# Ninth tap's projection inside the row-tile burst, and one TensorE loop over both axes, in an LSTM and deformable-sampling kernel

## The reference

```python
def dsc_axis(x, offset, weight, axis):
    off = jnp.transpose(offset, (0, 2, 3, 1))      # 9 offsets for each pixel
    if axis == 'x':
        ix = wb + off; iy = jnp.broadcast_to(hb, off.shape)
    else:
        iy = hb + off; ix = jnp.broadcast_to(wb, off.shape)
    s = grid_sample_zeros(x, ix, iy)               # linear between two pixels of the row or column
    return jnp.einsum('bchwk,ock->bohw', s, weight)
...
x = x + lstm_layer(_gn(x), ...)
x = x + conv_block(_gn(x), ...)
```

## Time and profile before

| | us |
|---|---|
| median of 3 runs | 934.19 (932.71 to 934.72) |
| the profiled execution, its own time | 935.11 |
| its span | 933.3 |
| TensorE busy, matmuls | 794.4 (85%) |
| TensorE busy, weight loads | 620.6 (66%) |
| VectorE busy | 635.0 (68%) |
| ScalarE busy | 522.8 (56%) |
| POOL busy | 114.3 (12%) |
| L868, `dist`, 4608 matmuls, busy | 219.8 |
| L914, `product`, 8192 matmuls (its further ones, with y8, are listed by themselves), busy | 194.2 |
| L881, `project`, 4096 matmuls, busy | 78.8 |
| L893, `project_last`, 2048 matmuls, busy | 67.6 |

### The profile page before, as it was taken

How to read it: one execution, slowest core, us unless ns; L and a number is a source line. 1 busy time by engine, 2 the same in 40 slices (tenths; PEclk the granted TensorE clock), 3 DMA queues, 4 the chain that set the end, 5 groups by cost and what they waited for, 6 DMA issues and landing times.

```text
span 933.3 us, 61844 instructions
## 1 busy us (share of the span) xinstructions
PE 794.4 (85%) x27560; PEld 620.6 (66%) x27560; DVE 635.0 (68%) x1472; ACT 522.8 (56%) x1044; POOL 114.3 (12%) x227
## 2 busy tenths in 40 slices
PE   0688888879779999779779999999979999999970
PEld 0455556555357777523468888889868888898860
DVE  4466666664622222377668888888868999999975
ACT  0344444440121111165668888888857888888854
POOL 0122222210000000000211111111111111111103
PEclk9999999985679999989999999999999999999995
DMA  8200000000000000000000000000000000000006
GB/s 213 81 2 1 0 1 0 0 1 1 3 2 4 4 4 4 3 2 1 3 3 0 0 0 0 0 0 0 1 5 1 0 0 0 0 0 0 0 3 180
DMA packets 4073, 12.15 MB, mean 13 GB/s; under 512 B 1391, under 2 KB 1787, under 8 KB 3460
## 3 DMA queue, kind: packets, MB, share of 16 engines
q1 hardware_dynamic: 1716, 4.88, 1.9%
q10 hardware_dynamic: 1522, 4.14, 1.6%
q0 software_dynamic: 768, 2.10, 0.8%
HBM read 6.92 MB, written 4.19 MB: 12 GB/s over the span
## 4 chain that ended last, share of the span: by engine, by line
PE 75%; DVE 11%; issue 6%; ACT 4%; DMA 2%; POOL 1%; ACTq 0%; DVEq 0%; POOLq 0%
PE psum L914 16%; PE psum L868 15%; PE psum L817 14%; PE psum L881 8%; PE psum L893 6%; PE psum L755 5%; PE psum L840 3%; PE psum L742 3%; DVE offs L637 2%; DVE wide L556 2%; PE psum L797 2%; DVE wide L559 2%; DMA xs<-in_x_dram 2%; ACT wide L382 1%; ACT wide L386 1%
## 5 line engine op out<-in xcount | busy, mean ns | idle before, releaser
L457 ACT ACTIVATE wide<-psum 128x512 f32<-128x512 f32 x576 | 304.0, 606 | 10.8 <-PE psum L868 10.7
L656 DVE TENSOR_SCALAR wide<-wide 128x512 f32<-128x512 f32 x576 | 246.6, 447 | 48.0 <-ACT wide L457 37.8
L868 PE MATMUL psum<-wide,sels 125*32 125x256 bf16 x4608 | 219.8, 275 | 4.2 <-issue 3.3
L914 PE MATMUL psum<-wide 128*32 128x64 f32 x8192 | 194.2, 219 | 9.4 <-issue 8.4
L914 PEld LDWEIGHTS psum<-wide 128*32 128x32 f32 x8192 | 168.5, 109 | 12.6 <-issue 11.0
L662 DVE COPY wide<-psum 128x512 f32<-128x512 f32 x192 | 131.5, 685 | 10.2 <-PE psum L881 10.1
L817 PE MATMUL psum<-img,offs 32*32 32x512 f32 x3456 | 126.7, 596 | 4.4 <-DVE img L610 4.4
L755 PEld LDWEIGHTS psum<-wide 128*64 128x64 f32 x2048 | 75.9, 140 | 66.5 <-issue 65.8
L817 PEld LDWEIGHTS psum<-img,offs 32*32 32x32 f32 x3456 | 96.0, 103 | 34.3 <-issue 7.9
L868 PEld LDWEIGHTS psum<-wide,sels 125*32 125x32 bf16 x4608 | 94.6, 97 | 25.3 <-issue 15.2
L755 PE MATMUL psum<-wide 128*64 128x64 f32 x2048 | 89.7, 229 | 21.7 <-DVE wide L567 19.4
(11 more groups left out here) (97 smaller groups left out, 821.2 us busy)
## 6 DMA issues: line engine op xcount, KB each, us to landing
xs<-in_x_dram SPq DMA_DIRECT2D x8, 256.0 KB, 9.8
xs<-in_x_dram ACTq DMA_DIRECT2D x8, 256.0 KB, 11.0
out_dram<-wide SPq DMA_DIRECT2D x16, 128.0 KB, 3.5
out_dram<-wide POOLq DMA_DIRECT2D x16, 128.0 KB, 4.0
offs<-in_cw_dram ACTq DMA_DIRECT2D x1, 576.0 KB
sels<-in_sel_dram ACTq DMA_DIRECT2D x1, 562.5 KB
wide<-in_dsc_dram ACTq DMA_DIRECT2D x1, 288.0 KB
offs<-in_dwd_dram ACTq DMA_DIRECT2D x1, 288.0 KB
```

The costliest lines, as they stand in the source:

```text
L457: nc.scalar.activation(hat_tile(par, i), ps[USE_BANK[u]].rearrange("p (q n) -> p q n", q=2), ACT.Abs).then_inc(d_read, 1)
L656: nc.vector.tensor_scalar(v, v, 1.0, 1.0, ALU.min, ALU.subtract).then_inc(v_ready, 1)
L868: last = mm(bank[c, e * SL:(e + 1) * SL], sels[:, k, c], oc[0:NROW, par, :], start=(e == 0), stop=(e == 1))
L914: last = mm(ps[O_BANK][C * q:C * q + C, cols], w, v, start=(group == 0), stop=(group == GROUPS - 1))
```

## The change

- `wm8` and `project_last` are gone. The ninth tap is now computed in `project`, in the same form as the other taps: weights are the pixels (64 columns), and the moving operand is the 32 columns of tap 8. There are 16 such matmuls (32 recorded) a slot, each 32 rows by 64 columns of the array. Groups 0 and 1 go in front of the other taps' matmuls of row tiles 0 and 1, groups 2 and 3 in front of those of row tiles 2 and 3. As groups 0 and 2 write the same partitions of the bank, and 1 and 3 likewise, TensorE waits for `y8_half`, the end of the first half, ahead of row tile 2.
- The ninth tap is use 0 (bank 0), the hats are uses 1 to 9. GROUPS_AFTER is new.
- ScalarE takes the ninth tap first, in two activations of 64 partitions by 256 columns, into alternate blocks of `y8`, then hat 0, then y of group 0, then hats 1 to 8. The blocks of `y8` that are never written are zeroed once by POOL at the start.
- TensorE's two loops are one of 31 rounds, for both axes, with two slots behind it. For this `project` always reads the weights of axis 0, and POOL, at the change of axis, waits until all slots of axis 0 are projected and copies the weights of axis 1 over them.

```diff
-        wm8 = region(2 * 2 * Q * C).rearrange("p (a e q n) -> p a e q n", a=2, e=2, q=Q)
...
-        USES, Y8_USE = 10, 4
+        USES, Y8_USE = 10, 0
...
+            nc.gpsimd.memset(y8[:, :, :, :, :], 0.0).then_inc(y8_zero, 1)
...
-            step(nc.gpsimd.memset(wm8, 0.0))
-            for a in range(2):
-                for q in range(Q):
-                    s_ = slice(C * q, C * q + C)
-                    last = nc.gpsimd.tensor_copy(wm8[s_, a, q % 2, q, :], wcv[s_, a, 8, :])
-            last.then_inc(wm_ready, 1)
-            pool.wait_ge(wm_ready, 1)
...
+                    if g0 == NCH:
+                        pool.wait_ge(y_ready, Q * 2 * NCH)
+                        step(nc.gpsimd.tensor_copy(wc[:, 0, :], wc[:, 1, :]))
...
+            act.wait_ge(y8_zero, 1)
             with act.Fori(0, 2 * NCH) as g:
                 for par in range(2):
-                    act.wait_ge(y_ready, g * (2 * Q) + (par * Q + 1))
-                    nc.scalar.activation(yt[:, par, 0, :, :], ps[Y_BANK[0]]..., ACT.Copy).then_inc(y_read_a, 1)
-                    for u in range(USES):
-                        if u == Y8_USE:
-                            act.wait_ge(y8_ready, g * 2 + (par + 1))
-                            nc.scalar.activation(y8[:, par, :, :, :], ps[USE_BANK[u]]..., ACT.Copy).then_inc(d_read, 1)
-                        else:
-                            ...
+                    act.wait_ge(y8_ready, g * 2 + (par + 1))
+                    for e in range(2):
+                        half = slice(S * e, S * e + S)
+                        last = nc.scalar.activation(y8[half, par, :, e:Q:2, :],
+                                                    ps[USE_BANK[Y8_USE]][half, 0:2 * HROWS * C].rearrange(
+                                                        "p (r q m) -> p r q m", r=HROWS, q=2), ACT.Copy)
+                    last.then_inc(d_read, 1)
+                    for i in range(HATS):
+                        act.wait_ge(d_ready, g * (2 * HATS) + (par * HATS + i + 1))
+                        nc.scalar.activation(hat_tile(par, i), ps[USE_BANK[hat_use(i)]]..., ACT.Abs).then_inc(d_read, 1)
+                        if i == 0:
+                            act.wait_ge(y_ready, g * (2 * Q) + (par * Q + 1))
+                            nc.scalar.activation(yt[:, par, 0, :, :], ps[Y_BANK[0]]..., ACT.Copy).then_inc(y_read_a, 1)
...
-            def project(a, s, slots, par):
+            def project(s, slots, par):
                 ...
+                free_bank(s, slots, Y8_USE)
                 for r in range(HROWS):
+                    pair = (0, 1) if r < 2 else (2, 3)
+                    if r == 2:
+                        pe.wait_ge(y8_half, s + (slots + 1))
+                    for r8 in (r * 2 % HROWS, r * 2 % HROWS + 1):
+                        for q in pair:
+                            c, e = slice(C * q, C * q + C), q % 2
+                            at = (2 * r8 + q // 2) * C
+                            last = mm(ps[USE_BANK[Y8_USE]][S * e:S * e + S, at:at + C], xc[c, par, r8 * S:(r8 + 1) * S],
+                                      wcv[c, 0, 8, :], start=(r8 == 0 and q < 2), stop=True, skip_group_check=True)
+                        if r8 == HROWS - 1:
+                            last.then_inc(y8_half if r < 2 else y8_ready, 1)
                     for e in range(2):
                         ...
-            def project_last(a, s, slots, par):
-                ...
-            GROUPS_AFTER = (0, 3, 3, 2, 1, 3, 3, 3, 2, 0)
+            GROUPS_AFTER = (0, 2, 2, 3, 2, 3, 2, 3, 3, 0)
...
-            pe.wait_ge(wm_ready, 1)
-            for a in range(2):
-                s0 = 2 * a * NCH
-                if a == 0:
-                    slot(a, s0, None, 1, True)
-                with pe.Fori(0, NCH - 1) as g:
-                    for par in range(2):
-                        slot(a, g * 2, s0 + par, par, True)
-                slot(a, 2 * NCH - 2, s0, 0, True)
-                slot(1, 2 * NCH - 2, s0 + 1, 1, a == 0)
+            slot(0, None, 1, True)
+            with pe.Fori(0, 2 * NCH - 1) as g:
+                for par in range(2):
+                    slot(g * 2, par, par, True)
+            slot(4 * NCH - 2, 0, 0, True)
+            slot(4 * NCH - 2, 1, 1, False)
```

More of the change, by code:

```diff
@@ L173, in build @@
                                                      for n in ("off_mm", "part1", "rest1", "part2", "rest2", "part3"))
-        wm_ready = sem("wm_ready")
+        y8_zero = sem("y8_zero"); y8_half = sem("y8_half")
         xc_ready = sem("xc_ready"); oc_ready = sem("oc_ready"); d_ready = sem("d_ready"); d_read = sem("d_read"); v_ready = sem("v_ready")
@@ L441, in _ @@
                 parts_x(rd)
+            act.wait_ge(y8_zero, 1)
             with act.Fori(0, 2 * NCH) as g:
                 for par in range(2):
-                    act.wait_ge(y_ready, g * (2 * Q) + (par * Q + 1))
-                    nc.scalar.activation(yt[:, par, 0, :, :], ps[Y_BANK[0]].rearrange("p (r m) -> p r m", r=HROWS),
-                                         ACT.Copy).then_inc(y_read_a, 1)
-                    for u in range(USES):
-                        if u == Y8_USE:
-                            act.wait_ge(y8_ready, g * 2 + (par + 1))
-                            nc.scalar.activation(y8[:, par, :, :, :],
-                                                 ps[USE_BANK[u]].rearrange("p (r q m) -> p r q m", r=HROWS, q=Q),
-                                                 ACT.Copy).then_inc(d_read, 1)
-                        else:
[L455 to L458, removed]
+                    act.wait_ge(y8_ready, g * 2 + (par + 1))
[7 more added lines that the diff above has]
+                        act.wait_ge(d_ready, g * (2 * HATS) + (par * HATS + i + 1))
+                        nc.scalar.activation(hat_tile(par, i), ps[USE_BANK[hat_use(i)]].rearrange("p (q n) -> p q n", q=2),
+                                             ACT.Abs).then_inc(d_read, 1)
+                        if i == 0:
+                            act.wait_ge(y_ready, g * (2 * Q) + (par * Q + 1))
+                            nc.scalar.activation(yt[:, par, 0, :, :], ps[Y_BANK[0]].rearrange("p (r m) -> p r m", r=HROWS),
+                                                 ACT.Copy).then_inc(y_read_a, 1)
             norm_sqrt(BNF, 1)
@@ L881, in project @@
                             last = mm(ps[Y_BANK[q]][S * e:S * e + S, r * P:(r + 1) * P], xc[c, par, r * S:(r + 1) * S],
-                                      wcv[c, a, e:8:2, :], start=(r == 0), stop=(r == HROWS - 1))
+                                      wcv[c, 0, e:8:2, :], start=(r == 0), stop=(r == HROWS - 1))
                             if e == 1 and r == HROWS - 1:
                                 last.then_inc(y_ready, 1)
-            def project_last(a, s, slots, par):
[L888 to L895, removed]
             GROUPS = HROWS * 5
-            GROUPS_AFTER = (0, 3, 3, 2, 1, 3, 3, 3, 2, 0)
+            GROUPS_AFTER = (0, 2, 2, 3, 2, 3, 2, 3, 3, 0)
             def product(s, slots, par, group):
@@ L916, in product, with slot @@
                     last.then_inc(out_ready, 1)
-            def slot(a, s, slots, par, ahead):
+            def slot(s, slots, par, ahead):
                 nslots = 0 if slots is None else slots + 1
@@ L923, in slot @@
                     pe.wait_ge(oc_ready, s + (nslots + 1))
-                    project(a, s, nslots, 1 - par)
+                    project(s, nslots, 1 - par)
                 for u in range(USES):
[L926 to L929, removed]
+                    if ahead and u != Y8_USE:
+                        dist(s, nslots, 1 - par, u - 1)
                     if slots is not None:
```

## The result

The changed kernel took 956.95 us in the median (948.42 to 963.38, 4 runs), the kernel before 934.46 (932.71 to 936.55, 4 runs). The recorded ratio is 1.016, 95% interval 1.0119 to 1.0202; in a second series on another chip it is 1.0353, 1.0255 to 1.0450. Executions fall on two levels some 14 us apart (before 933.5 or 920.3, after 963.3 or 949.5), and the recorded ratio compares the changed kernel's two executions at the lower level (950.65 and 948.42) with executions of the kernel before that are all at the upper one, whereas at one and the same level the change costs 29 to 30 us, 3.2%. The cleanest measure is the sampling itself, from the first burst's start to the last's: 442.87 us before, 470.13 after, +27.3; a second profile of the changed kernel gives 470.07. The profiled execution took 963.25 us against 935.11, +28.1.

The account below looks back on a forecast made before the run. TensorE and ScalarE were taken to be near the limit together, ScalarE's chain setting the new slot. 60 slots at +0.28 gave +16.8 us, one loop -11.7: together +5.1, 939.3 us against the median 934.19; range 914 to 952, forecast's own 931 to 947.

Parts of the forecast that it names:

- One loop, -11.7: At the change of axis, TensorE's stalls on the first pass through new code vanish with one loop: -11.7 us.
- The burst ends at 2.03 and grows by 0.82: TensorE's burst of ninth tap and `project`, at 57 ns a ninth-tap pass, ends at 2.03 us instead of 1.21.
- ScalarE starts the ninth tap at 1.84: ScalarE starts 1.84 us after the burst's start, when the last ninth-tap pass is done and seen.
- Each half activation takes 0.29, hat 0 starts at 2.42: ScalarE's two 256-column ninth-tap activations take 0.58 us in place of 0.50, so hat 0 can start at 2.42.
- Seven steps to hat 6, 3.36: On ScalarE, hat 0, the copy of y and hats 1 to 5 take 0.48 us each, 3.36 in all.
- Hat 6 itself 0.61: ScalarE's hat 6, which frees the bank for the last `dist`, takes 0.61 us.
- 0.33 from the last dist to the burst: At the slot's end, the next burst starts 0.33 us after the last `dist` starts.
- The moved waits: TensorE's `free_bank` ahead of the burst and `y_ready` behind hat 0 find their events past: cost 0.
- cheap passes: Rival: a ninth-tap pass costs its 27 ns of streaming, the burst grows by 0.37, 913.5 us; chance 27%.
- TensorE alone counts: Rival: ScalarE catches up, so TensorE's time sets the slot at 6.44 us, 919.5 us total; chance 10%.
- strict order: Rival: array tiles don't pass each other, the burst ends at about 2.2, slot 6.95, 949.5 us; chance 19%.
- The rule of program order: Skill's rule: TensorE matmuls stay in program order, only weight loads are pulled ahead; ninth-tap passes would hold back other tiles.

Follow-up runs that it names:

- after_again: The changed kernel run once more, unchanged, as the reference on the same chip: median 963.3 us, sampling 470.07 us.
- wide_tap: The changed kernel with 64 columns streamed in each ninth-tap matmul in place of 32: median 959.95 us, sampling 473.92 us.
- no_free: The changed kernel without the `free_bank` wait at the head of `project`: median 957.88 us, sampling 465.46 us.
- half_act: The changed kernel with only the first of the two ninth-tap activations, TensorE's work the same: median 951.01 us, sampling 458.12 us.
- spread_lean: The kernel before with one TensorE loop, two product groups moved behind the ninth tap's projection, and no wait for `oc` at the slot's head: median 925.99 us.

## Why the prediction was right and wrong

The direction and the mechanism were right, the size was not: +5.1 us was forecast and 28.1 measured in the profiled executions. The stated range of 914 to 952 held the recorded outcome (1.016 times 934.46 is 949.4), but that is luck: it hangs on which executions that ratio compares. The 963 us of the profiled execution and of `after_again` lie outside the range, and the forecast's own range of 931 to 947 held neither value. Step by step:

- *One loop, -11.7*: right. It is 11.70 alone, 11.0 of it at the change of axis. Undone in the changed kernel it is 8.7, so there the rest of the change costs 36 and not 39.
- *The burst ends at 2.03 and grows by 0.82*: right. It is 2.06, +0.85. `wide_tap` shows that the streamed columns are not the price of a pass; the weight load as the price fits but was not varied.
- *ScalarE starts the ninth tap at 1.84*: right, 1.85 (598.80 - 596.95).
- *Each half activation takes 0.29, hat 0 starts at 2.42*: this step failed. The second half starts 0.39 after the first (0.77 less its 0.38) and hat 0 0.40 after that, so hat 0 starts at 2.64, +0.22. I had taken off the overlap that activations of 512 columns show. What was measured, 0.39 and 0.40, is above even the upper bound of 0.375 that stood in the prediction. Why these halves do not overlap is open.
- *Seven steps to hat 6, 3.36*: right (599.59 to 602.95). *Hat 6 itself 0.61*: 0.67, +0.06. In the unbroken row hats start 0.48 apart but each ends a little later; their mean rose to 630 ns from 606.
- *0.33 from the last dist to the burst*: 0.41, +0.08. This step failed too. The moved waits were costed at nothing because their events are past. `no_free` shows what one of them costs anyway: an instruction of the sequencer, 0.07 to 0.10.
- These three terms are 0.36, and 6.78 + 0.36 = 7.14: the slot is explained to 0.01. Odd slots take 0.02 more. Over 60 slots (14.74 - 13.44) / 2 = 0.65 is 39 us; less 11.7 that leaves 27.3, the measured growth of the sampling.

Of the rivals, *cheap passes* fell with the burst and `wide_tap`; *TensorE alone counts* with `half_act`; *strict order* gave 949.5, the figure nearest to the recorded ratio, but by a burst of 2.2 that isn't there, so its nearness is luck as well. The rule of program order that the prediction took from the Trainium skill ("TensorE: Matmul & The Clock Gate", step-by-step part of Part 2) does not hold between tiles in this trace. The eight ninth-tap passes of a row tile stand ahead of the other taps' in the program, yet the first L894 starts at 597.09 while the last of these L887 start at 597.14. The sum that lets the tiles run past each other hit the burst to 0.03. What was foreseen of the two waits of TensorE, ahead of `dist` 4 and of the last `dist`, is in the profile.

The share of each cause follows from the chain, laid beside that of the kernel before (6.49 to 7.13). ScalarE starts its row 1.85 after the burst's start in place of 1.19, as it waits for the last ninth-tap pass of the longer burst: +0.66, the largest part. From there to the end of hat 6 it takes 4.82 in place of 4.92: -0.45 for the old stop ahead of the ninth tap, +0.29 for two activations in place of one, +0.06 for the longer hat 6. The path from there to the next burst is 0.07 longer. The sum is 0.63 of the 0.64. The prediction says that one step before hat 6 is gone; that is wrong, though its sum does not use it: the same eight pieces (the ninth tap, the copy of y, hats 0 to 5) stand ahead of hat 6 in both kernels.

## What to carry to other kernels

Two engines that hand banks to each other can both be near the limit: take the slot apart from the event that closes it, back to the burst, and price a change on that chain before counting what it saves on the busier engine. Work that moves to a place where the other engine stands idle, waiting for it, lengthens the loop by itself: here the burst grew by 0.85 us and ScalarE's start moved by 0.66. And look at which read the last use waits for: here another bank for one use gave 16 us without moving any work.

## What was not expected of the hardware

- An activation of 64 partitions by 256 columns costs 0.39 to 0.40 us on the path, against 0.48 to 0.50 for 128 by 512, so two halves cost 0.79 for 0.50. The activations of 512 columns overlap (0.60 long, 0.48 apart), the halves do not (0.38 long, 0.39 apart).
- Each instruction of TensorE's sequencer ahead of a burst takes 0.09 to 0.11 us while the array is idle, also a wait whose event is past (`no_free`: 0.07 to 0.10 a slot). Two waits that share an instruction cost one (even slots of `spread_lean`).
- An fp32 pass behind a weight load of 64 columns takes 0.058 us on its tile with 32 or 64 streamed columns alike (`wide_tap`).
- Matmuls on different tiles of the array start out of program order (L894 at 597.09, L887 at 597.14).
